# Who writes the scaled attention output of a tile: VectorE (before) or ScalarE (after)

## The reference

```python
xn   = layernorm(x)
# attention: scores from xn and W_qk, linear position bias, causal mask
scores = einsum('bqe,bke->bqk', xn @ W_qk, xn) * SCALE + (kpos - qpos) * slope
attn = softmax(where(qpos >= kpos, scores, -inf))
s    = einsum('bqk,bkd->bqd', attn, xn @ W_v.T)
# mixture of experts: 8 experts, each token goes to its top one, 512 slots an expert
g    = silu(ffn(xn, Wr, W1, W2))
out  = x + s * g
```

## Time and profile before

| | |
|---|---|
| median of three runs | 481.29 us |
| the profiled execution | 480.52 us |
| its span, first to last instruction | 478.8 us |
| around the span | 1.72 us |
| TensorE busy | 438.9 us, 92% |
| VectorE busy | 333.8 us, 70% |
| ScalarE busy | 213.8 us, 45% |
| GpSimd busy | 202.5 us, 42% |
| mean granted TensorE clock | 0.973 of full |

### The profile page before, as it was taken

One profiled execution on the slowest core, in us unless ns is written; L12 is line 12 of the kernel. 1 busy time (PEld: TensorE's weight loads), 2 busy tenths in 40 slices (PEclk: granted clock), 3 DMA queues, 4 the chain that ended last, 5 costly groups with the idle time before them and its releaser, 6 DMA issues.

```text
span 478.8 us, 8483 instructions
## 1 busy us (share of the span) xinstructions
PE 438.9 (92%) x3138; PEld 302.9 (63%) x3138; DVE 333.8 (70%) x881; ACT 213.8 (45%) x396; POOL 202.5 (42%) x337
## 2 busy tenths in 40 slices
PE   4777999999999979999999999999999999999960
PEld 1444576676677756766776787666666666666640
DVE  4779576878667767876765654779696887967330
ACT  1443354453354454554435443455555545545320
POOL 4106654415050563823041000346658485755751
PEclk9899899999999989999999999999999999999995
DMA  6982825303500536624002406348758475734030
GB/s 215 342 332 69 211 78 145 121 1 80 172 27 1 165 112 167 220 58 166 2 17 66 93 11 220 90 143 201 200 164 255 115 259 184 212 78 130 23 120 33
DMA packets 64312, 63.42 MB, mean 132 GB/s; under 512 B 36902, under 2 KB 58156, under 8 KB 62224
## 3 DMA queue, kind: packets, MB, share of 16 engines
q1 hardware_dynamic: 53472, 40.78, 29.2%
q0 software_dynamic: 5632, 16.73, 11.0%
q10 hardware_dynamic: 5168, 5.37, 3.4%
HBM read 30.29 MB, written 25.43 MB: 116 GB/s over the span
## 4 chain that ended last, share of the span: by engine, by line
PE 70%; DVE 13%; ACT 5%; issue 3%; POOL 3%; DMA 2%; SPq 1%; POOLq 0%; DVEq 0%; ACTq 0%
PE bank L1119 18%; PE bank L1121 17%; PE bank L1120 17%; PE bank L1190 5%; PE bank L1205 4%; PE bank L1208 4%; PE bank L1207 4%; DVE sc L808 2%; ACT sc L1027 2%; DVE pT_l L824 2%; DMA sc<-in_w_r 1%; DVE stats L660 1%; POOL xn L530 1%; SPq L395 1%; ACT xnr L1001 1%
## 5 line engine op out<-in xcount | busy, mean ns | idle before, releaser
L1033 ACT ACTIVATE pT_h<-bank 128x512 f16<-128x512 f32 (+2 forms) x80 | 42.3, 530 | 84.9 <-PE bank L1190 84.5
L824 DVE SCALAR_TENSOR_TENSOR pT_l<-bank,pT_h 128x512 f16<-128x512 f32 (+2 forms) x80 | 48.6, 608 | 43.9 <-ACT pT_h L1033 42.6
L1205 PE MATMUL bank<-v_h,pT_h 128*128 128x257 f16 x272 | 74.9, 275 | 0.6 <-DVE pT_l L824 0.6
L1208 PE MATMUL bank<-v_h,pT_l 128*128 128x257 f16 x272 | 74.3, 273 | 0.0
L1207 PE MATMUL bank<-v_l,pT_h 128*128 128x256 f16 x272 | 73.9, 272 | 0.0
L1119 PE MATMUL bank<-w_h,hid_h 128*128 128x256 f16 x256 | 69.8, 273 | 0.0
L1121 PE MATMUL bank<-w_h,hid_l 128*128 128x256 f16 x256 | 69.8, 273 | 0.0
L1120 PE MATMUL bank<-w_l,hid_h 128*128 128x256 f16 x256 | 69.8, 273 | 0.0
L1045 ACT ACTIVATE hid_h<-bank 128x512 f16<-128x512 f32 x64 | 38.0, 594 | 70.3 <-PE bank L1121 70.3
L885 DVE SCALAR_TENSOR_TENSOR hid_l<-bank,hid_h 128x512 f16<-128x512 f32 x64 | 43.8, 684 | 34.9 <-ACT hid_h L1045 34.9
L1119 PE MATMUL bank<-xT,qT_h 128*128 128x512 f16 (+3 forms) x160 | 55.6, 351 | 5.7 <-DVE cmin L808 4.2
(11 more groups left out here) (168 smaller groups left out, 903.0 us busy)
## 6 DMA issues: line engine op xcount, KB each, us to landing
raw<-in_w_e SPq DMA_DIRECT2D x5, 2048.0 KB, 8.1
sc<-in_w_e SPq DMA_DIRECT2D x3, 2048.0 KB, 7.8
slots<-empty ACTq DMA_DIRECT2D x1, 4224.0 KB, 26.1
out<-xg SPq DMA_DIRECT2D x8, 512.0 KB, 3.3
rows<-xg SPq DMA_DIRECT2D x8, 512.0 KB, 4.2
rows<-so SPq DMA_DIRECT2D x8, 512.0 KB, 5.0
xg<-in_x SPq DMA_DIRECT2D x6, 512.0 KB, 4.7
xg<-in_x ACTq DMA_DIRECT2D x2, 512.0 KB, 6.0
```

Source lines behind the costliest of these rows:

```text
L824: v.scalar_tensor_tensor(pT_l[:, t % 2, cols], tr_ps[n % 2][:, 0:w], P_UP, pT_h[:, t % 2, cols], ALU.mult, ALU.subtract).then_inc(pT_lo, 1)
L1033: a_.activation(pT_h[:, t % 2, c * GTOK:c * GTOK + w], tr_ps[n % 2][:, 0:w], ACT.Copy, scale=P_UP).then_inc(pT_hi, 1)
L1205: pe.matmul(pv_ps[t % 2][:, 0:D + 1], pT_h[:, t % 2, rows_], v_h[:, at, q, 0:D + 1], start=kb == 0, stop=False)
L1208: last = pe.matmul(pv_ps[t % 2][:, 0:D + 1], pT_l[:, t % 2, rows_], v_h[:, at, q, 0:D + 1], start=False, stop=kb == t % NT)
```

## The change

After the change VectorE's `finish` computes the reciprocal and then one small product, 128 x 1: the reciprocal times `value_mul`. It signals a new semaphore, `s_mul_made`. A new `finish` in ScalarE's list waits for it and writes `so` with one activation (a copy with a scale that is read per partition). ScalarE signals `s_made`. The wait for the store of an earlier group (`rows_s`) moves with the write. In ScalarE's list the call stands right behind `high` and ahead of `probs`. For the last tile it stands between the first two `hidden`.

```diff
+        s_mul = sb("s_mul", [P, 2])
+        s_mul_made = sem("s_mul_made")
             def finish(t):                                  # VectorE
-                k, g = t % 2, t // GT
+                k = t % 2
                 dve.wait_ge(pv_full, t + 1)
                 step(v.reciprocal(rinv[:, k:k + 1], pv_ps[k][:, D:D + 1]))
-                if t % GT == 0 and g >= 2:
-                    dve.wait_ge(rows_s[g % 2], g // 2 * 16)
-                v.tensor_scalar(so[g % 2][:, t % GT, :], pv_ps[k][:, 0:D], rinv[:, k:k + 1], value_mul[:, 0:1],
-                                ALU.mult, ALU.mult).then_inc(s_made, 1)
+                v.tensor_scalar(s_mul[:, k:k + 1], rinv[:, k:k + 1], value_mul[:, 0:1], None, ALU.mult
+                                ).then_inc(s_mul_made, 1)
...
+            def finish(t):                                  # ScalarE
+                k, g = t % 2, t // GT
+                act.wait_ge(s_mul_made, t + 1)
+                if t % GT == 0 and g >= 2:
+                    act.wait_ge(rows_s[g % 2], g // 2 * 16)
+                a_.activation(so[g % 2][:, t % GT, :], pv_ps[k][:, 0:D], ACT.Copy, scale=s_mul[:, k:k + 1]
+                              ).then_inc(s_made, 1)
...
                     if c < chunks(t):
                         high(t, c)
+                    if c == chunks(t - 1) - 1:
+                        finish(t - 1)
                     ahead = min(chunks(t + 1), 2) if last_step(t, c) and (c or t % GT != 1) else 0
                     if ahead:
                         probs(t + 1, range(ahead))
...
-            for f in range(LEAD):
-                hidden(f, f)
+            hidden(0, 0)
+            finish(TILES - 1)
+            hidden(1, 1)
```

## The result

The kernel after takes 489.99 us (median of four runs, 489.20 to 493.54) against 480.72 us for the kernel before (479.85 to 482.09). The ratio is 1.0202, with a 95% interval of 1.0173 to 1.0232: slower, by 9.3 us between the medians, 9.7 us by the ratio. Forecast were 9.7 us more and 491.0 us. The profiled execution took 489.88 us, with a span of 488.2 against 478.8 us.

What follows compares the result with a forecast made beforehand. TensorE, busy 92% of the span, was taken to set the time. Delays at the tiles summed to 10.7 us, less 1.0 of VectorE's relief: +9.7 us, 491.0 us, with 8 in 10 between 486 and 495.5.

Steps and rivals of the forecast that it cites:

- The wait costs, not the work: ScalarE stops behind `high` for VectorE's low half, reciprocal and product, delaying `probs`; its added instruction costs nothing extra.
- The signs named: Profile after: write about 0.48 us, exponential waits 6 us or more, read waits about 9, VectorE's busy time down 10.6.
- The formula of 0.64 us from the product's start: Product 0.21, signal 0.04, activation 0.475, less overlap 0.09: 0.64 us from the product's start until `probs` can start.
- Tiles 6, 10, 14, 18, 22, 30: Late exponentials, or splits and projections behind them, reach TensorE: 1.2, 1.3, 1.4, 1.1, 1.2 and 1.4 us lost.
- The split's path: Late exponentials push ScalarE's split, that pushes VectorE's, and VectorE's reads of scores come later; at tile 10, 1.3 us.
- Tile 21: TensorE already waits 0.20 us for this exponential, which moves by 1.0 us.
- Tiles 1 and 2: ScalarE waits for a lagging VectorE, `v_l` starts late, and so does the transfer TensorE awaits at 53 us: 1.8 us.
- Tiles 15 to 17: Up to 0.7 us of delay ahead of TensorE's longest wait, 2.4 us, which hangs on GpSimd: no loss.
- VectorE's relief: VectorE gains 0.33 us a tile, counting only at tiles 11, 27 and ahead of 13: 1.0 us taken off.
- Tiles with a margin: Tiles 5, 9, 13, 25, 26, 29: margins of 0.1 us or so, less at 9 and 26; 0.3 us in all.
- Experts and last tile: The last 160 us of experts hold nothing of the change; at the last tile TensorE is in expert 0's second `up`.
- The rival with more falls: Waits near 158 and 184 us bring two or three more clock falls, 3.4 to 5.1 us, for 495 us; chance 0.12.

Runs made afterwards that it cites:

- the wait alone: Kernel before, VectorE still writing the output, but ScalarE waits for that write at the new write's place and does no work there: 491.53 us against 480.09, ratio 1.0226.
- the work alone: Kernel before plus a ScalarE activation of the same size at the new write's place, waiting for nothing: 481.77 us against 480.09, ratio 1.0021.
- the experiment: Kernel before without VectorE's 128 x 256 write, only reciprocal and 128 x 1 product left, no engine writing the output: 479.06 us against 480.09, ratio 0.9971.
- the uncovered tiles alone: Against the kernel before, ScalarE writes at tiles 1, 2, 5, 6, 9, 10, 13-18, 21, 22, 25, 26, 29, 30 and the last: 491.84 us against 480.70.

## Why the prediction was right, step by step

- **The wait costs, not the work.** Right: 10.8 us for the wait alone, 1.0 us for the work alone.
- **The signs named.** The write's 0.474 us, the 6 us or more of waits for exponentials (6.6 us from 36 us on) and TensorE's waits grown by over 5 us (by 8.0) came as forecast. VectorE's busy time fell by 9.5 us, not 10.6. The waits for VectorE's reads went from 4.2 to 5.7 us and not to about 9: part of the delay showed instead as waits for VectorE's routing, which grew from 1.2 to 3.8 us.
- **The formula of 0.64 us from the product's start.** Right to 0.02 us: at tile 30, 291.69 - 291.07 = 0.62 us. At tile 21 it is the same:

```profile
205.37 0.21 DVE L834 TENSOR_SCALAR s_mul<-rinv,value_mul 128x1 f32<-128x1 f32 x1
...
205.61 0.47 ACT L1042 ACTIVATE so<-bank,s_mul 128x256 f32<-128x256 f32 x1 [1.06 <-DVE s_mul L834]
205.99 1.22 ACT L1026 ACTIVATE sc<-sc,rmin 128x512 f32<-128x512 f32 x2
```

- **Tiles 6, 10, 14, 18, 22, 30.** Forecast 1.2, 1.3, 1.4, 1.1, 1.2 and 1.4 us; the lag grows by 1.15, 1.25, 1.43, 1.07, 1.14 and 1.43 us. The split's path is right too: TensorE had no wait after tile 10. Now it has one of 0.86 us for a read of VectorE's, and lost 0.2 us more at the transposes ahead of it (110.29 against 106.77 with a lag of 3.36):

```profile
115.06 0.39 PE L1131 MATMUL bank<-xT,qT_h 128*128 128x512 f16 x1 [0.86 <-DVE cmin L810]
```

- **Tile 21.** Forecast 1.0 us, and the lag grows by 1.03 us from tile 21 to 22. VectorE's relief at tile 20 had taken 0.33 us off just before (from 6.47 to 6.14 us), which I had not counted.
- **Tiles 1 and 2.** Forecast 1.8 us. `v_l` of tile 2 starts at 43.98 instead of 42.50, 1.48 us late. This execution was 0.22 us ahead at tile 1, so the two tiles took 1.7 us. By tile 5 the lag is 2.2 us, since TensorE's wait for the transfer grew from 1.0 to 1.7 us. This wait is not steady: in the twelve experiments it is between 1.1 and 2.8 us, also in kernels that leave these tiles alone. The clock just before goes with it. In the five traces in which TensorE runs at full clock from 44 us to this wait it is 2.6 to 2.8 us; in the other nine, with the granted clock at 0.50 for part of that time, it is 1.0 to 2.0 us. Where TensorE got there sooner, it waited longer for the same transfer.

```profile
42.58 0.47 ACT L1042 ACTIVATE so<-bank,s_mul 128x256 f32<-128x256 f32 x1 [2.17 <-DVE s_mul L834]
...
43.98 0.42 DVE L774 SCALAR_TENSOR_TENSOR v_l<-bank,v_h 128x256 f16<-128x256 f32 x1 [1.43 <-ACT v_h L1015]
```

- **Tiles 15 to 17: nothing.** Right in sum (5.38 us at tile 15, 5.28 at 18), by the way that was forecast: the lag rises to 6.26 us, and TensorE's long wait for GpSimd's work takes it back, falling from 2.4 to 1.6 us.
- **VectorE's relief.** Tiles 11 and 12 gave 0.32 and 0.33 us, tile 27 0.34 us. Missed were tile 28, where 0.24 us came back in the same way as at tile 12, and tile 20 above. The term was 1.0 us, and the experiment says 1.4. This term was somewhat too small.
- **Tiles with a margin.** Forecast 0.3 us together; tile 26 took 0.22 us, the others nothing.
- **Experts and last tile: nothing.** Right: the lag is 9.38 us at tile 31, 9.38 at the last tile and 9.4 at the end of the span.
- **The clock.** The rival with more falls did not come. There is one fall in this part of the kernel after as before, but it moved. In the kernel before it came behind the wait at 174 us. Windows of the kernel after (length, busy time of the engines, granted clock):

```profile
186.00:188.00 2.00, 0.97 (x7) 0.45 (x5) 1.21 (x6) 0.96 (x3) 0.00 (x0) 1.00 0.42 82
188.00:190.00 2.00, 0.96 (x14) 0.72 (x14) 1.86 (x9) 1.32 (x3) 0.00 (x0) 0.82 0.87 149
190.00:192.00 2.00, 1.40 (x4) 0.57 (x5) 1.93 (x9) 0.47 (x1) 0.26 (x2) 0.50 1.01 343
192.00:194.00 2.00, 2.00 (x14) 1.21 (x13) 0.31 (x2) 1.63 (x3) 1.51 (x8) 0.82 0.31 103
```

TensorE was under half busy from 186 to 190 us before the clock went to 0.50, which is 1.2 GHz. The Trainium skill's reading (the page "TensorE: Matmul & The Clock Gate", section "HAM oscillation — how this bites in real kernels"), that waits between bursts bring the slow clock back, fits this place. In this execution it doesn't make the sum short: from tile 19 to tile 21 the lag falls. In the experiments with the wait alone and with the uncovered tiles alone the same fall lasted longer and did cost, as the last section shows. So it is in part luck that the rival took nothing here.

## What to carry to other kernels

Before an instruction is moved to a less busy engine, ask what its input waits for and what is queued behind its new place. A wait in a strictly ordered list delays everything behind it, and the engine's idle share says nothing about that. Here the place in the list was worth 8 us and the work 1 us. If the input comes late, put the instruction behind all that someone waits for; if that isn't possible, make the input earlier, in time in which its engine waits anyway.

## What the runs showed of the hardware that was not expected

**A slow clock that cost nothing, and one that cost its price.** I had priced a fall at 1.7 us. In the kernel before, TensorE ran at 0.50 from 178 to 180 us. In the version with ScalarE at the first and fourth tiles it ran at full clock in the same part:

```profile
178.00:180.00 2.00, 2.00 (x18) 1.47 (x16) 1.85 (x5) 0.83 (x3) 0.00 (x0) 1.00 0.20 41
180.00:182.00 2.00, 2.00 (x17) 1.49 (x15) 1.95 (x7) 1.06 (x3) 0.00 (x0) 1.00 0.48 95
182.00:184.00 2.00, 0.89 (x16) 0.55 (x14) 1.80 (x9) 1.32 (x3) 0.00 (x0) 1.00 0.58 121
```

It gained nothing by it. It was through with its matmuls earlier and then waited, 1.06 us for the routing and 0.90 us for a read of VectorE's, where the kernel before waited 0.61 us in all. VectorE is busy for 1.8 us or more of 2 in each window: it sets the pace there.

The other side is in the kernel with the wait alone. The fall behind the wait for the routing, the one shown above for the kernel after, lasted longer there:

```profile
190.00:192.00 2.00, 1.85 (x5) 0.74 (x6) 1.84 (x9) 0.00 (x0) 0.39 (x2) 0.50 1.00 340
192.00:194.00 2.00, 2.00 (x10) 1.08 (x8) 0.34 (x1) 1.63 (x3) 1.50 (x8) 0.50 0.01 2
194.00:196.00 2.00, 2.00 (x14) 1.65 (x13) 1.08 (x3) 0.06 (x1) 0.95 (x4) 0.67 0.38 57
```

The first of these windows is at 0.50 in both kernels. From 192 to 196 us TensorE is busy all the time and VectorE a third of it, and the granted clock is 0.50 and 0.67 against 0.82 and 1.00 in the kernel after. From tile 19 to tile 20 the lag grows by 1.6 us here, by 0.1 us in the kernel after. The kernel with the uncovered tiles alone shows the same (0.50 and 0.62, 1.6 us). So a fall costs where TensorE sets the pace, and only there.

The clock also goes with the scatter between runs. Of 29 runs of the kernel before, the four with a mean granted clock of 0.965 took 482.1 to 482.3 us, the nine with 0.981 or more 479.0 to 480.3 us. A good part of the scatter is there before the change can act: at tile 1 the traces of the other kernels lie from 0.9 us ahead of the kernel before to 1.6 us behind it.

**A GpSimd instruction that starts inside a certain VectorE one takes longer by nearly the rest of it.** GpSimd's four normalising instructions near 170 us took 5.30 against 4.94 us when ScalarE wrote the output of tiles 15 and 16 later in its list. One of the four makes the difference, the one that starts while VectorE writes `w_l` (line 867 before, line 866 in this kernel; 128 x 512 from two SBUF tiles, 0.75 us). In the kernel with the write at the end of the tile:

```profile
171.28 0.75 DVE L866 SCALAR_TENSOR_TENSOR w_l<-raw,wup,w_h 128x512 f16<-128x512 f32 x1 [0.28 <-ACT w_h L1048]
```

GpSimd's second instruction starts at 171.47 us, with 0.56 us of `w_l` left, and takes 1.65 us. In the kernel before `w_l` starts at 170.87 and the instruction at 171.42, with 0.20 us left, and it takes 1.30 us. The same holds between 132 and 138 us in all fourteen traces and near 171 us in ten of them: with 0.55 to 0.60 us left it takes 1.65 to 1.70 us, with 0.19 to 0.23 us left 1.28 to 1.32 us, and started outside `w_l` 1.21 to 1.24 us. So what ScalarE's list changed is when the two meet. In the other four traces, the kernel after among them, `w_l` starts second there, GpSimd's instructions take 1.21 to 1.23 us, and `w_l` takes 0.81 to 0.89 us instead of 0.75. Why one holds up the other no run here shows.
